# Attention B of a hybrid kernel: another order of the engines in projections, head and tail, and the keys' low halves on POOL

## The reference

```python
q = (resid @ Wq).reshape(B, T, 32, 16).transpose(0, 2, 1, 3)
k = (resid @ Wk).reshape(B, T, 8, 16).transpose(0, 2, 1, 3)
v = (resid @ Wv).reshape(B, T, 8, 16).transpose(0, 2, 1, 3)
q = q * cos + rotate_half(q) * sin
k = k * cos + rotate_half(k) * sin
att = einsum('bhgqd,bhkd->bhgqk', q.reshape(B, 8, 4, T, 16), k) / sqrt(16)
probs = softmax(where(causal, att, -inf))
out = einsum('bhgqk,bhkd->bhgqd', probs, v)  # back to B, T, 512
return out @ Wo
```

## Time and profile before

| | us |
|---|---|
| median of 3 runs (lowest, highest) | 1044.24 (1041.33, 1045.87) |
| the profiled execution | 1044.38 |
| its span, first to last instruction | 1042.5 |
| TensorE busy (93%) | 965.8 |
| VectorE (DVE) busy (77%) | 804.2 |
| ScalarE (ACT) busy (60%) | 620.6 |
| GpSimd (POOL) busy (56%) | 580.4 |

### The profile page before, as it was taken

The page is one execution under the profiler, slowest core; times in us unless marked ns, Lnnn a source line. Parts: engine busy times, 40 slices in busy tenths (PEclk is TensorE's granted clock), DMA queues, the critical chain, the costliest instruction groups (busy, mean ns, idle before and its releaser), DMA issues.

```text
span 1042.5 us, 21597 instructions
## 1 busy us (share of the span) xinstructions
PE 965.8 (93%) x7715; PEld 533.3 (51%) x7715; DVE 804.2 (77%) x1869; ACT 620.6 (60%) x1362; POOL 580.4 (56%) x570
## 2 busy tenths in 40 slices
PE   3698999999999999999999999689987799998998
PEld 1244555555555555555555555345555455554554
DVE  5877887887887887887887888767867888882744
ACT  2267666666666666666666655444377488886131
POOL 3768876876886876876876873143655011110111
PEclk9989999999999999999999999899999699999999
DMA  8164475374475374475374374400000000000002
GB/s 288 48 194 123 87 198 132 76 197 131 77 197 131 76 197 131 77 191 133 81 197 131 77 158 137 91 1 2 1 1 2 1 2 3 3 2 2 1 1 81
DMA packets 179895, 95.48 MB, mean 92 GB/s; under 512 B 168032, under 2 KB 168544, under 8 KB 175200
## 3 DMA queue, kind: packets, MB, share of 16 engines
q1 hardware_dynamic: 170016, 49.64, 22.1%
q10 hardware_dynamic: 9792, 44.59, 13.2%
HBM read 50.17 MB, written 2.10 MB: 50 GB/s over the span
## 4 chain that ended last, share of the span: by engine, by line
PE 74%; DVE 9%; POOL 5%; ACT 5%; issue 5%; DMA 1%; SPq 0%; ACTq 0%; DVEq 0%; POOLq 0%
PE bank L986 14%; PE bank L987 14%; PE bank L988 14%; PE bank L1386 4%; PE bank L1073 3%; PE bank L1075 3%; PE bank L1074 3%; PE bank L1093 3%; PE bank L1095 3%; PE bank L1094 3%; PE bank L1329 2%; PE bank L1310 2%; PE bank L1334 2%; PE bank L1295 1%; DVE bank L1584 1%
## 5 line engine op out<-in xcount | busy, mean ns | idle before, releaser
L501 POOL TENSOR_TENSOR rt<-rt 128x512 f32<-128x512 f32 x80 | 101.1, 1267 | 137.9 <-DVE rt L1569 137.9
L1601 DVE SCALAR_TENSOR_TENSOR bw_hi<-bank,rden,bw_hi 128x128 f16<-128x128 f32 (+3 forms) x256 | 123.3, 544 | 61.4 <-ACT bw_hi L765 61.4
L734 ACT ACTIVATE bank<-bank,shift,c_score 128x128 f32<-128x128 f32 (+3 forms) x256 | 147.3, 605 | 2.1
L1584 DVE CUSTOM_DVE_ANT_0 bank<-bank,mask_w 128x512 f32<-128x512 f32 (+3 forms) x256 | 118.1, 520 | 21.6 <-PE bank L1075 21.3
L765 ACT ACTIVATE bw_hi<-bank,rden 128x128 f16<-128x128 f32 (+3 forms) x256 | 114.5, 536 | 25.3 <-DVE rden L1594 25.2
L729 ACT ACTIVATE shift<-smax,c_score 128x4 f32<-128x4 f32 x64 | 19.0, 297 | 163.4 <-DVE smax L1584 163.4
L986 PE MATMUL bank<-xt,wq_hi 128*128 128x512 f16 x256 | 99.2, 387 | 2.2 <-DVE rt L1569 1.8
L746 ACT ACTIVATE pt<-bank,c_score_b 128x512 f32<-128x512 f32 x128 | 81.1, 686 | 29.7 <-PE bank L1295 29.7
L987 PE MATMUL bank<-xt,wq_hi 128*128 128x512 f16 x256 | 98.7, 385 | 0.0
L988 PE MATMUL bank<-xt,wq_lo 128*128 128x512 f16 x256 | 98.5, 385 | 0.0
L986 PE MATMUL bank<-wo_hi,arena 128*128 128x512 f16 x256 | 97.5, 381 | 0.6 <-DVE x L1613 0.6
(11 more groups left out here) (234 smaller groups left out, 2619.6 us busy)
## 6 DMA issues: line engine op xcount, KB each, us to landing
qcode<-in_q_codes ACTq DMA_DIRECT2D x8, 1024.0 KB, 5.0
qscale<-in_q_scales ACTq DMA_DIRECT2D x8, 1024.0 KB, 8.0
ocode<-in_o_codes ACTq DMA_DIRECT2D x7, 1024.0 KB, 4.9
oscale<-in_o_scales ACTq DMA_DIRECT2D x7, 1024.0 KB, 8.8
kvcode<-in_k_codes ACTq DMA_DIRECT2D x8, 256.0 KB, 8.7
kvcode<-in_v_codes ACTq DMA_DIRECT2D x8, 256.0 KB, 9.0
kvscale<-in_k_scales ACTq DMA_DIRECT2D x8, 256.0 KB, 8.9
kvscale<-in_v_scales ACTq DMA_DIRECT2D x8, 256.0 KB, 9.2
```

The lines of the kernel that those rows point to most:

```text
L734: act.activation(a_rows(i, s), a_rows(i, s), ACT.Exp, bias=shift[:, s % 2, c:c + 1], scale=c_score[:, 0:1], accum_out=bank[3][:, SUMS_AT + ...
L1584: dve.tensor_tensor_reduce(bank[bk][:, o:o + (i + 1) * P], bank[bk][:, o:o + (i + 1) * P], mask_w[:, S - (i + 1) * P:S], 1.0, LOWEST, ALU. ...
L1601: dve.scalar_tensor_tensor(out=p_row[:, s % 2, LO_AT[i]:LO_AT[i] + P_STEP * i + 1:P_STEP], in0=turned_back(i, s), scalar=rden[:, s % 2, c: ...
```

## The change

The stack gets another order: a query head's pieces are high, high, low, low, a key head's four times high, low, so that `k_stack` doubles to 512 elements of each half and the keys take two units, 4 and 5, of full height. POOL makes the low halves of all queries and, behind them, all keys; DVE none. ACT copies units 0, 1, 4 and 5 of tiles 0 to 5 and all units of tiles 6 and 7 (which use banks 4 and 7), DVE units 2 and 3 of tiles 0 to 5. TensorE's b_q is cut in three, with units 2 to 5 of the tile before last between the parts; units 0 and 1 of the last tile come at the end of the round. The units of tiles 6 and 7 that are left then lie between the first scores; set 0's six steps come before set 1's, and set 1's first four lie around set 0's turned maxima. In the tail the first two tiles of the result are turned and split beside the last set's product with the values, and tile 0's product with Wo follows it. `...` stands where lines are left out; the other edits of `stack_high` change the views only.

```diff
-B_STEPS = [(0, 0, 3), (0, 0, 2), (0, 0, 1), (0, 1, 3)]
-for _q in range(SETS):
+B_STEPS = [(0, 0, 3), (0, 0, 2), (0, 0, 1), (0, 1, 3), (0, 1, 2), (0, 1, 1), (1, 0, 2), (0, "max", 0), (1, 0, 3),
+           (1, 0, 1), (1, 1, 3)]
+for _q in range(1, SETS):
...
+UNITS = 6
+ACT_UNITS = (0, 1, 4, 5)
+
+
+def t_bank(t, unit):
+
+    return ((2, 7) if t < NT - 2 else (4, 7))[unit % 2]
+
+
+def act_units(t, unit):
+
+    before = len(ACT_UNITS) * min(t, NT - 2) + UNITS * max(t - (NT - 2), 0)
+    return before + (unit + 1 if t >= NT - 2 else ACT_UNITS.index(unit) + 1)
+
+
+def dve_units(t, unit):
+
+    return 2 * t + unit - 1
...
-                if t < NT - 1:
-                    pool.wait_ge(bq_hi, t + 1)
-                    st = q_stack[:, i2].rearrange("p (h e a d) -> p h e a d", h=B_HEADS, e=2, a=2)
-                    rq = rq1[:, i2].rearrange("p (h d) -> p h d", d=B_HD).unsqueeze(2)
-                    pool.tensor_tensor(st[:, :, :, 1], rq.broadcast_to([P, B_HEADS, 2, B_HD]), st[:, :, :, 0],
-                                       ALU.subtract).then_inc(bq_lo, 1)
+                pool.wait_ge(bq_hi, t + 1)
+                st = q_stack[:, i2].rearrange("p (h a e d) -> p h a e d", h=B_HEADS, a=2, e=2)
+                rq = rq1[:, i2].rearrange("p (h d) -> p h d", d=B_HD).unsqueeze(2)
+                pool.tensor_tensor(st[:, :, 1], rq.broadcast_to([P, B_HEADS, 2, B_HD]), st[:, :, 0],
+                                   ALU.subtract).then_inc(bq_lo, 1)
+                pool.wait_ge(bk_hi, t + 1)
+                st = k_stack[:, i2].rearrange("p (h e a d) -> p h e a d", h=KV_HEADS, e=4, a=2)
+                rk = rk1[:, i2].rearrange("p (h d) -> p h d", d=B_HD).unsqueeze(2)
+                pool.tensor_tensor(st[:, :, :, 1], rk.broadcast_to([P, KV_HEADS, 4, B_HD]), st[:, :, :, 0],
+                                   ALU.subtract).then_inc(bk_lo, 1)
...
+            def stack_out(t, units):
+
+                for w in units:
+                    act.wait_ge(bt_ps, UNITS * t + w + 1)
+                    if (t, w) == (0, 4):
+                        act.wait_ge(zeros_done, 4)
+                    to, c = (qt_b, 4 * w) if w < 4 else (kt_b, 4 * (w - 4))
+                    act.activation(to[:, c:c + 4, t * P:(t + 1) * P],
+                                   bank[t_bank(t, w)][:].rearrange("p (c n) -> p c n", c=4), ACT.Copy).then_inc(bt_act, 1)
 
             ln_hi(2, 0)
             ln_hi(2, 1)
             for t in range(NT):
-                if t:
-                    q_out(t - 1)
-                stack_high(t)
+                if t >= 2:
+                    stack_out(t - 2, (4, 5))
                 if t + 2 < NT:
                     ln_hi(2, t + 2)
                 if t:
-                    k_out(t - 1)
-            q_out(NT - 1)
-            k_out(NT - 1)
+                    stack_out(t - 1, (0, 1))
+                stack_high(t)
+            stack_out(NT - 2, range(2, UNITS))
+            stack_out(NT - 1, range(UNITS))
...
+                if q == SETS:
+                    m_high(NT, 1.0)
+                    m_high(NT + 1, 1.0)
...
+                    if t >= NT - 2:
+                        held = (t, w - 2) if w >= 2 else (t - 1, w + 4)
+                        pe.wait_ge(bt_act, act_units(*held))
+                    elif w < 2 and t:
+                        pe.wait_ge(bt_act, act_units(t - 1, w + 4))
+                    elif w in (2, 3):
+                        pe.wait_ge(bt_act, act_units(t, w - 2))
+                    elif w >= 4:
+                        pe.wait_ge(bt_dve, dve_units(t, w - 2))
...
-                wide(bank[t % 2][:], t, "b_q", D).then_inc(bq_ps, 1)
-                if t:
-                    stack_t(t - 1, (0, 1))
+                wide(bank[t % 2][:], t, "b_q", D, range(0, 1))
+                if t >= 2:
+                    stack_t(t - 2, (2, 3))
+                wide(bank[t % 2][:], t, "b_q", D, range(1, 3))
+                if t >= 2:
+                    stack_t(t - 2, (4, 5))
+                wide(bank[t % 2][:], t, "b_q", D, range(3, 4)).then_inc(bq_ps, 1)
+                if t + 2 < NT:
+                    ln_t(2, t + 2)
                 if t >= 2:
                     pe.wait_ge(bv_done, t - 1)
                 wide(bank[5 + t % 2][:, 0:2 * P], t, "b_kv", 2 * P).then_inc(bkv_ps, 1)
                 if t:
-                    stack_t(t - 1, (2, 3))
-                if t + 2 < NT:
-                    ln_t(2, t + 2)
-                if t:
-                    stack_t(t - 1, (4,))
+                    stack_t(t - 1, (0, 1))
...
-            pe.wait_ge(bt_act, 3 * ST)
-            pe.wait_ge(bt_dve, 2 * ST)
+            stack_t(NT - 2, (2, 3))
+            pe.wait_ge(bt_act, act_units(NT - 3, UNITS - 1))
+            pe.wait_ge(bt_dve, dve_units(ST - 1, 3))
             pe.wait_ge(bq_mul, NT)
             b_scores(0, 0, 3)
-            stack_t(NT - 1, range(5))
-            pe.wait_ge(bt_act, 3 * (NT - 1) + 2)
-            pe.wait_ge(bt_dve, 2 * NT)
             b_scores(0, 0, 2)
             b_scores(0, 0, 1)
+            stack_t(NT - 2, (4, 5))
             b_scores(0, 1, 3)
-            pe.wait_ge(bt_act, 3 * NT)
+            stack_t(NT - 1, (0, 1))
+            b_scores(0, 1, 2)
+            stack_t(NT - 1, range(2, UNITS))
+            b_scores(0, 1, 1)
+            pe.wait_ge(bt_act, act_units(NT - 1, UNITS - 1))
+            pe.wait_ge(bt_dve, dve_units(NT - 3, 3))
             pe.wait_ge(bv_done, NT)
+            b_scores(1, 0, 2)
+            b_turn_max(0)
+            b_scores(1, 0, 3)
+            b_keys(0, 0)
+            b_scores(1, 0, 1)
+            b_scores(1, 1, 3)
...
+                if q == SETS:
+                    turn(NT, ctx_b[:, 0], bctx, 2 * KV_HEADS - 1)
+                    turn(NT + 1, ctx_b[:, 1], bctx, 2 * KV_HEADS - 1)
...
+                if q == SETS:
+                    second(NT, "b_o")
...
             ln_norm(2, 2)
             for t in range(NT):
-                if t:
-                    kv_low(t - 1)
+                if t + 3 < NT:
+                    ln_norm(2, t + 3)
+                if t >= 2:
+                    stack_out(t - 2)
                 dve.wait_ge(bq_ps, t + 1)
                 if t >= 2:
-                    dve.wait_ge(bq_lo, t - 1)
+                    dve.wait_ge(bk_lo, t - 1)
                 rope_products(bank[t % 2][:], rq1[:, t % 2], rq2[:, t % 2], t).then_inc(bq_mul, 1)
+                if t + 2 < NT:
+                    ln_lo(2, t + 2)
                 dve.wait_ge(bkv_ps, t + 1)
                 rope_products(bank[5 + t % 2][:, 0:P], rk1[:, t % 2], rk2[:, t % 2], t).then_inc(bk_mul, 1)
-                if t:
-                    stack_out(t - 1)
-                if t + 2 < NT:
-                    ln_lo(2, t + 2)
-                if t + 3 < NT:
-                    ln_norm(2, t + 3)
-
-            dve.wait_ge(bq_hi, NT)
-            st = q_stack[:, (NT - 1) % 2].rearrange("p (h e a d) -> p h e a d", h=B_HEADS, e=2, a=2)
-            rq = rq1[:, (NT - 1) % 2].rearrange("p (h d) -> p h d", d=B_HD).unsqueeze(2)
-            dve.tensor_tensor(st[:, :, :, 1], rq.broadcast_to([P, B_HEADS, 2, B_HD]), st[:, :, :, 0],
-                              ALU.subtract).then_inc(bq_lo, 1)
-            kv_low(NT - 1)
-            stack_out(NT - 1)
...
+            b_max(0, 0, 3)
+            b_max(0, 0, 2)
+            b_max(0, 0, 1)
             b_max(0, 1, 3)
-            for q in range(-1, SETS + 2):
+            b_max(0, 1, 2)
+            b_max(0, 1, 1)
+            b_max(1, 0, 2)
+            b_max_out(0)
+            b_max(1, 0, 3)
+            b_max(1, 0, 1)
+            b_max(1, 1, 3)
...
-            m_low(NT, 1.0)
+                if q == SETS:
+                    m_low(NT, 1.0)
+                    m_low(NT + 1, 1.0)
```

More of the change, by code:

```diff
@@ L323, in build @@
         q_stack = staged("q_stack", [P, 2, B_HEADS * B_ST], F16)
-        k_stack = staged("k_stack", [P, 2, KV_HEADS * B_ST], F16)
+        k_stack = staged("k_stack", [P, 2, KV_HEADS * 2 * B_ST], F16)
         stage.close()
@@ L921, in stack_high @@
                 act.wait_ge(bq_rot, t + 1)
-                st = q_stack[:, i2].rearrange("p (h e a d) -> p h e a d", h=B_HEADS, e=2, a=2)
+                st = q_stack[:, i2].rearrange("p (h a e d) -> p h a e d", h=B_HEADS, a=2, e=2)
                 rq = rq1[:, i2].rearrange("p (h d) -> p h d", d=B_HD).unsqueeze(2)
-                act.activation(st[:, :, :, 0], rq.broadcast_to([P, B_HEADS, 2, B_HD]), ACT.Copy).then_inc(bq_hi, 1)
+                act.activation(st[:, :, 0], rq.broadcast_to([P, B_HEADS, 2, B_HD]), ACT.Copy).then_inc(bq_hi, 1)
                 act.wait_ge(bk_rot, t + 1)
-                st = k_stack[:, i2].rearrange("p (h e a d) -> p h e a d", h=KV_HEADS, e=2, a=2)
+                st = k_stack[:, i2].rearrange("p (h e a d) -> p h e a d", h=KV_HEADS, e=4, a=2)
                 rk = rk1[:, i2].rearrange("p (h d) -> p h d", d=B_HD).unsqueeze(2)
```

(26 more changed lines are left out.)

18 lines of the change are left out of this document (4 added, 14 removed).

## The result

The changed kernel takes 1035.3 us (median of 6, 1031.45 to 1035.71) beside 1043.94 (6 runs, 1040.56 to 1047.18); the ratio is 0.9916, interval 0.9897 to 0.9936. It is faster by 8.6 us, where 12 were forecast. The profiled execution took 1035.46, its span is 1033.7.

What follows compares the result with a forecast made beforehand. No engine was full in a projection round; chains of waits between engines closed it. Gains of 5.7 (projections), 5.6 (head) and 1.7 (tail) made 13.0, less 0.5 for handing over: 12.5 off 1044.38, so 1032 us, range 1028 to 1038.5.

Steps and rivals of the forecast that it cites:

- a second set's copy more than 26 us after E: Sign of a wrong forecast, in attention B's head: second set's turned maxima copied more than 26 us after E.
- E: End of b_q of tile 7, closing the projections: forecast at 795.1, before at 800.9.
- the head's second part: Attention B's head, first to second copy of turned maxima: 10.7 us forecast, 9.97 before, so 0.7 given back.
- The projections: Projection stage up to E: denser rounds and an earlier start of b_q were to gain 5.7 us.
- The round: One tile of the projections: forecast 5.95 us, from TensorE's work of 5.70 and a wait of 0.25.
- a wait of 0.25 ahead of unit 3: In each projection round, TensorE waits 0.25 us for ACT's copy to free the bank of unit 1.
- The keys' low halves: POOL's added 512-element subtraction in each projection round, priced at 1.16 us.
- the ring: Projections: POOL's add, ACT's high halves, POOL's low halves of queries and keys in a loop, 5.7 us a round.
- The shared port: Rival, projections: DVE's subtraction L1477 meets POOL's 2.13 us instruction, copies 1.6 us late; 1038 us, chance 0.05.
- The head's first part: Attention B's head, E to the first set's turned maxima: forecast E + 14.2, a gain of 6.3 us.
- the second rival: Attention B's head stays slow, TensorE at half clock: copies E + 17.4 and 11.3 later; 1035 us, chance 0.10.
- The tail: Attention B's end: two TensorE waits ahead of b_o's first product vanish, gaining 1.7 us.

Runs made afterwards that it cites:

- the last experiment: Changed kernel with one unit per quarter of b_q, second key step earlier, and resultless matmuls in head and tail; 1028.35 us, ratio 0.9855.
- POOL's part alone: Kernel before with one edit: POOL makes the keys' low halves behind the queries', DVE none; 1043.46 us, ratio 0.9995.
- the orders alone: Changed kernel with the keys' low halves back on DVE, ahead of its wait for b_q; 1039.91 us, ratio 0.9957.
- both mended: Changed kernel with resultless matmuls keeping TensorE busy in the head and set 0's second key step earlier; 1029.63 us, ratio 0.9862.
- finer units: Changed kernel with units 2 to 5 one each behind a quarter of b_q instead of in pairs; 1032.22 us, ratio 0.9898.

## Why the prediction was right, and where it was off

1032 was forecast, with 1028 to 1038.5 around it; 1035.3 was measured. The direction and the mechanism were right, the size was not: 8.6 us of a forecast 12. One of the prediction's own signs of being wrong came true: it named a second set's copy more than 26 us after E, and that copy ended 27.0 us after E (13.6 + 13.5). This points at the head's second part, below.

**The projections: right, term by term.** E came 5.7 us sooner relative to the stage's start, as walked. The round was put at 5.95 from TensorE's 5.70 and a wait of 0.25 ahead of unit 3; measured 5.93 and 0.26, and the wait is shown by its removal (5.68). The keys' low halves were put at 1.16 (measured 1.15) and the ring at 5.7 (5.64, seen in the last experiment). The rounds needed both parts together: with POOL's part alone they stayed at 6.5 to 6.6 in the mean, with the orders alone at 6.46.

**The shared port: right in kind, once in the way.** L1503 (the subtraction that was L1477 before) met POOL's add of 770.11 once, showed 1.59 us and ended 0.28 behind it, and this round took 6.32. That is 0.4 us in all, in the round that was walked at 5.97. When DVE's subtraction was put where POOL's 2.13 us lie, the rival came out at its full size, 2.21 us for an instruction that shows 0.68 elsewhere. In the changed kernel it does not decide.

**The head's first part: 7.2 for 6.3.** The step from E to the first copy was put at 14.2 and took 13.6, which hides a part of the miss behind it.

**The step that failed is the one up to the second set's copy.** I took 10.7 us between 9.5 at full and 11.3 at half clock; it took 13.5. The half clock was there, as the second rival had it, but its price was too low: even the 11.3 went by a stretch whose mean clock was 0.61, and here it was 0.50. TensorE's order was left out: the second key step stood behind score steps waiting for DVE, so TensorE first waited for DVE (0.53 and 0.37 us) and then DVE for TensorE, 3.6 us in three gaps. At full clock the same order takes 11.35, so the clock is worth 2.1 us and is most of the 2.8 missed; the order is worth 1.1 at the low clock and 0.4 at full clock. With both mended the step takes 10.99, still 1.5 above the 9.5 that I had summed from DVE's work, and where those lie isn't shown. So the head gave 3.7 us, not 5.6. The second rival, 1035 by a later first and second copy, would have hit the total by luck, by other terms: the first copy was not late at all.

**The tail: 2.1 to b_o, less 0.5 behind it, for 1.7.** The transposes that moved behind b_o's first product were not counted on the way there.

**The rest of the miss** is the stage ahead of the change. It was 2.1 us later in the changed kernel's profile; whether the timed runs had as much of that can't be read.

## What to carry to other kernels

When an order is made denser, price the busiest engine's queue too: what stands behind each waiting instruction, on both sides. Here one 512-element subtraction fitted into the slack of one engine and cost half a microsecond a round where it met the other's long instruction. And where TensorE has gaps that can't be closed, as in a head that waits for another engine, a few matmuls with no result in the gaps may keep its clock; look at the granted clock of that stretch before and after, and don't count a later stretch's clock as their gain. In the kernel before, such matmuls brought the clock back sooner in the profile, and the timings showed no gain.

## What was not expected

The clock's fall is not bound to the place that caused it before: TensorE fell to half clock at 810.6 in the changed kernel, at 803.6 with finer units, at 817.1 with seven matmuls added, and not at all with seventeen. In the tail the same instructions ran at 0.88 in the changed kernel (14.4 us from the last copy to b_o) and at 1.00 in the run with seventeen (12.9): another 1.5 us that no edit of the tail made. The matmuls in the head 130 us earlier are not needed for it: the run with POOL's keys' low halves made twice has no matmul added and shows the same 12.9 us at 1.00. The kernel before shows the same in its tail, 16.5 us at 0.90 and 15.2 at 1.00 in the run with only the keys' low halves moved to POOL. What decides there isn't shown.
